# A decoder kernel on one core: the batch loop of both attention layers turned by half, and a key tile's second maximum placed behind the second head's scores

## What is computed

```
# layer 0: attention, no mask, two gates
aperture, expression = sigmoid(x @ Wa + ba), sigmoid(x @ We + be)       # per row and head
attn = softmax((x @ Wi) (x @ Wo)^T / sqrt(dh)) * aperture[q] * expression[k]
attn = attn / (attn.sum(-1) + 1e-8)
out  = rotate(attn @ (x @ Wv)) @ Wout          # a rotation and gains per head, folded into Wout
x    = layernorm(x + out)
# layer 1: attention of x over ctx, with a mask and biases
attn = softmax(where(mask == 0, -1e9, (x Wq^T + bq)(ctx Wk^T + bk)^T / sqrt(dh)))
x    = layernorm(x + (attn @ (ctx Wv^T + bv)) Wo^T + bo)
# layer 2: 16 experts with causal attention
...
```

## Time and profile before

| what | value |
|---|---|
| median of 3 runs | 4911.23 us |
| lowest, highest | 4908.39, 4921.2 us |
| the profiled execution | 4916.44 us, span 4914.7 us |
| TensorE busy, share of the span | 4307.2 us, 88% |
| VectorE, ScalarE, GpSimd busy | 2653.4 (54%), 1568.2 (32%), 902.7 us (18%) |
| granted clock of TensorE, mean | 0.935 |
| layer 0, layer 1, experts, about | to 1848, to 3845, to the end |

### The profile page before, as it was taken

How to read it: one execution, slowest core, us unless ns; L and a number is a source line. 1 busy time by engine, 2 the same in 40 slices (tenths; PEclk the granted TensorE clock), 3 DMA queues, 4 the chain that set the end, 5 groups by cost and what they waited for, 6 DMA issues and landing times. The chain is left out here.

```text
span 4914.7 us, 64052 instructions
## 1 busy us (share of the span) xinstructions
PE 4307.2 (88%) x22296; PEld 2467.3 (50%) x22296; DVE 2653.4 (54%) x3552; ACT 1568.2 (32%) x2813; POOL 902.7 (18%) x616
## 2 busy tenths in 40 slices
PE   5997899789879976999799979997999599989897
PEld 4443643454364434443544354435443376768686
DVE  3563465256345633664466445644664675757584
ACT  1453155225514531343134313431344202020302
POOL 3213311322132223102210221023101100000000
PEclk9999899899989997999899989998999799999898
DMA  3221322222122215210521052105210400010100
GB/s 84 67 65 50 80 47 61 69 65 46 46 83 67 53 37 159 61 40 27 168 61 40 27 168 61 40 27 163 65 40 18 140 18 35 18 35 7 46 1 18
DMA packets 120770, 294.79 MB, mean 60 GB/s; under 512 B 18352, under 2 KB 20272, under 8 KB 120432
## 3 DMA queue, kind: packets, MB, share of 16 engines
q1 hardware_dynamic: 93920, 222.20, 17.4%
q10 hardware_dynamic: 26512, 68.16, 4.1%
HBM read 145.87 MB, written 43.25 MB: 38 GB/s over the span
## 5 line engine op out<-in xcount | busy, mean ns | idle before, releaser
L869 ACT ACTIVATE probs<-half 128x512 f32<-128x512 f32 x2048 | 1113.2, 594 | 1176.0 <-PE half L682 679.8
L677 PE MATMUL half<-stack 97*128 97x512 f32 x2048 | 864.9, 487 | 9.9 <-ACT probs L869 5.6
L1044 DVE TENSOR_REDUCE mx<-wide 128x1 f32<-128x1024 f32 x512 | 603.0, 1220 | 443.2 <-PE wide L643 435.2
L1040 DVE CUSTOM_DVE_ANT_0 wide<-wide,mask_q 128x1024 f32<-128x1024 f32 x512 | 620.1, 1246 | 349.0 <-PE wide L643 341.4
L643 PE MATMUL wide<-stack 96*128 96x512 f32 x2048 | 630.5, 424 | 90.4 <-DMA stack<-qk 35.6
L677 PEld LDWEIGHTS half<-stack 97*128 97x128 f32 x2048 | 371.5, 192 | 600.9 <-issue 373.9
L609 PE MATMUL acc<-probs,v 128*32 128x512 f32 x4096 | 551.4, 609 | 2.9 <-ACT u L855 2.9
L587 PE MATMUL half<-stack,w 128*128 128x512 f32 x1536 | 388.6, 415 | 175.8 <-DVEq L953 151.7
L1386 PE MATMUL work_e<-w_in_e,x_e 128*128 128x512 f32 x2304 | 523.5, 389 | 0.0
L643 PEld LDWEIGHTS wide<-stack 96*128 96x128 f32 x2048 | 384.4, 192 | 200.4 <-DVE mx L1040 52.4
L1386 PEld LDWEIGHTS work_e<-w_in_e,x_e 128*128 128x128 f32 x2304 | 432.2, 188 | 89.7
(11 more groups left out here) (228 smaller groups left out, 3943.7 us busy)
## 6 DMA issues: line engine op xcount, KB each, us to landing
stack<-qk SPq DMA_DIRECT2D x384, 256.0 KB, 4.6
stage<-x_t SPq DMA_DIRECT2D x32, 512.0 KB, 3.5
k_raw<-x SPq DMA_DIRECT2D x8, 2048.0 KB, 9.3
x_t<-xts ACTq DMA_DIRECT2D x16, 1024.0 KB, 7.2
x<-k_raw ACTq DMA_DIRECT2D x8, 2048.0 KB, 8.6
mstage<-mask ACTq DMA_DIRECT2D x32, 512.0 KB, 3.6
mstage<-mask_t ACTq DMA_DIRECT2D x32, 512.0 KB, 3.6
over_a<-over_aperture SPq DMA_DIRECT2D x128, 64.0 KB, 2.7
```

Source lines behind the costliest of these rows:

```text
L677: last = pe.matmul(bank[:, :], stack[0:3 * DH + 1, s, 2 + h, kt * P:(kt + 1) * P], stack[0:3 * DH + 1, s, h, c * CH:(c + 1) * CH], start=T ...
L869: act.activation(probs[:, kt % 2 * 2 + h, c * CH:(c + 1) * CH], bank[:, :], ACT.Exp, scale=SCALE).then_inc(free, 1)
L1040: dve.tensor_tensor_reduce(bank[:, :], bank[:, :], mask_q[:, t, :], 1.0, -3e38, ALU.add, ALU.max, mx[:, p % 2, n:n + 1]).then_inc(free, 1)
L1044: dve.tensor_reduce(mx[:, p % 2, n:n + 1], bank[:, :], AX.X, ALU.max).then_inc(free, 1)
```

## The change

`attention_steps` is replaced by `pair_steps` and `section_steps`, which make three lists instead of one. Section 0 is the projections of batch 0. Section 1, in `Fori(0, B - 1)`, is the pair loop of batch i and then the projections of batch i + 1, woven with the end of batch i. Section 2 is the last pair loop and its end. `Section`, `Count` and `Ring` count, for each semaphore and buffer, how often it has been used up to a step of a section; they emit no instruction. The text of the engines is in a function `run(sec)` that goes through a section's list.

In the pair loop `MAXIMA` gives how many maxima stand in each tile, and only the first stands between the heads; the others (`late`) stand behind the second head's scores. `SLOT` gives each pair's place in `stack`: 0, 1, 2, 0, 1, 2, 1, 0. Pair 7's maxima but the last nine come ahead of pair 6's, and pair 7's stack ahead of pair 6's. Pairs 6 and 7 then have few or no maxima to work ahead on, and slots 1 and 2 become free for the next batch's x.

```diff
+SLOT = (0, 1, 2, 0, 1, 2, 1, 0)
...
+MAXIMA = ((2, 3, 3, 3, 3, 3, 2, 2),) + ((2,) * 8,) * 4 + ((2, 3, 3, 3, 3, 3, 1, 0), (2, 2, 2, 2, 1, 0, 0, 0), (0,) * 8)
...
+def pair_steps(masked, nxt):
+
+    units = lambda p: [("sm", p, h, t) for h in range(2) for t in range(TT)]
+    ahead = [m for p in range(1, 6) for m in units(p)] + units(7)[:7] + units(6) + units(7)[7:]
...
     for p in range(PAIRS):
         for kt in range(TT):
             before = (p, kt - 1) if kt else (p - 1, TT - 1)
+            if kt == 0 and p in (1, 2, 3, 4, 5):
+                steps.append(("stack", {1: 3, 2: 4, 3: 5, 4: 7, 5: 6}[p]))
+            if kt == 1 and p in (1, 3):
+                steps.append(("group", p // 2 + 2))
+            if nxt and kt == 1 and p == 5:
+                steps += [("load", "wv", 0), ("load", "wv", 1), ("split", "wv", 0), ("split", "wv", 1)]
+            if nxt and kt == 0 and p == 6:
+                steps += [("load", "xk", 0), ("load", "xk", 1)]
+                if masked:
+                    steps += [("mload", 0), ("mload", 1)]
+            if nxt and kt == 0 and p == 7:
+                for k in range(KT):
+                    steps.append(("split", "xk", k))
+                    if k < 2:
+                        steps.append(("load", "xk", k + 2))
             steps += [("st", p, kt, 0, c) for c in range(NC_)]
             misc = due
             due = []
...
-            spread = bool(ahead)
-            maxima(2 if p or kt else 0)
-            if not spread and before[0] >= 0:
+            rate = MAXIMA[p][kt]
+            late = []
+            for n in range(rate):
+                m = ahead.pop(0)
+                if n >= 1:
+                    late.append(m)
+                    continue
+                steps.append(m)
+                if m[2:] == (1, TT - 1):
+                    due.append(("mneg", m[1]))
+            if not rate and before[0] >= 0:
                 steps.append(("pv", *before, 0))
             steps += [("st", p, kt, 1, c) for c in range(NC_)]
             steps += misc
-            if p == 0 and kt:
-                maxima(1)
+            for m in late:
+                steps.append(m)
+                if m[2:] == (1, TT - 1):
+                    due.append(("mneg", m[1]))
...
+            if not masked and nxt and p == 7 and kt in (5, 6):
+                steps.append(("EX", kt - 5))
+            if masked and nxt and p == 7:
+                steps += [("mask", kt), ("mload", kt + 2)]
...
-    steps += [("out", t) for t in range(TT)]
-    steps += [("xt", t) for t in range(TT)]
...
+def section_steps(masked, att, nxt):
...
+    if att:
+        steps += pair_steps(masked, nxt)
+        steps.append(("res",))
+    else:
+        if masked:
+            steps += [("mload", 0), ("mload", 1)]
+        steps += [("load", "xk", 0), ("load", "wv", 0), ("split", "xk", 0), ("split", "wv", 0)]
+        steps += [("load", "xk", 1), ("load", "wv", 1), ("split", "xk", 1), ("split", "wv", 1)]
+        steps += [("load", "xk", 2), ("load", "xk", 3), ("split", "xk", 2), ("split", "xk", 3)]
+        if masked:
+            steps += [m for n in range(TT) for m in (("mask", n), ("mload", n + 2))]
+        else:
+            steps += [("turn_in",), ("EX", 0), ("EX", 1)]
...
+        for t in range(TT):
+            steps.append(("V", t))
+            if masked:
+                steps += [("mask", TT + t)] + ([("mload", TT + t + 2)] if t < TT - 2 else [])
+            steps += tail[t]
+        steps += [("load", "wk", 0), ("load", "wk", 1)]
...
+    if att:
+        if masked:
+            steps.append(("bo",))
+        steps += [("ct", t) for t in range(4)]
+        for t in range(TT):
+            if nxt and t < 2:
+                steps += [("split", "wk", t), ("load", "wq", t)]
+            steps.append(("out", t))
+            if t + 4 < TT:
+                steps.append(("ct", t + 4))
...
+        if masked:
+            steps += [("load", "xq", 0), ("load", "xq", 1)] + both("K", 0) + store
+            steps += both("K", 1) + both("K", 2) + both("K", 3)
+            for k in range(KT):
+                steps += [("split", "xq", k)] + ([("load", "xq", k + 2)] if k < 2 else [])
+            steps += [("xt", t) for t in range(HALF)] if att else []
+            steps += both("Q", 0) + stacked + both("Q", 1) + both("Q", 2)
+            steps += with_maxima(both("Q", 3) + [("CS", n) for n in range(4)], (3, 3, 3, 3, 2, 2))
+        else:
+            steps += both("K", 0) + store + both("K", 1) + both("Q", 0) + stacked + both("Q", 1) + both("K", 2)
+            steps += with_maxima(both("Q", 2) + both("K", 3) + both("Q", 3), (3, 3, 3, 3, 2, 2))
+        assert not first
+        steps += [("stack", 1), ("mneg", 0), ("row", 0)]
+        if att:
+            steps += [("xt", t) for t in range(HALF if masked else 0, TT)]
...
-        y = k_raw[:, :, :].rearrange("p g (a d) -> p (g a) d", d=D)
+        ct = sb("ct", [P, 4, 2, D], F32R, at=place["k_raw"])
...
+        y = sb("y", [P, TT, D], at=place["probs"])
+        wkv = sb("wkv", [P, 2, KT, D], F32R, at=place["qk"] if masked else None)
...
+                    elif kind == "res":
+                        sp.wait_ge(pv_done, blocks.upto(sec, ("pv", PAIRS - 1, TT - 1, 1)))
+                        alone(sp)
+                        sp.dma_start(y[:, :, :], io["res"][sec.batch, :, :].rearrange("b (t p) d -> p (b t) d", p=P))\
+                          .then_inc(res_in, 16)
...
-                    if kind == "out":
-                        pe.drain().then_inc(out_done, 1)
...
+            run(Section(0, None, False, True, lists[0]))
+            with dve.Fori(0, B - 1) as i:
+                run(Section(1, i, True, True, lists[1]))
+            run(Section(2, None, True, False, lists[2]))
```

1218 lines of the change are left out of this document (647 added, 571 removed).

## The result

The changed kernel took 5009.9 us (median, 5004.2 to 5016.3) against 4909.9 of the kernel before, a ratio of 1.020 (95% interval 1.0187 to 1.0212). It is 100 us slower where 41 less was forecast, and lies 75 us above the top of the stated range (4935). Its profiled execution has a span of 5014.3 us against 4914.7, so the two traces hold the whole difference.

A forecast was written before the change was run, and what follows sets the result against it. TensorE was taken as busy in key tiles and waiting in six inner boundaries, 1,003 us together. Layer 0's terms gave -8 and layer 1's -33, together -41 from 4911.2: 4870 us, range 4800 to 4935.

The forecast's parts named there:

- Tiles: Pair-loop key tiles: a maximum moved behind the second head's scores costs 0.46 us; +18.2 a batch in layer 0, +3.7 in layer 1.
- rival A: Pair-loop tiles: the late maximum is free, as the second head's exp holds `pv` anyway; 4776 us, chance 0.10.
- Tile 0 and the stall behind it: Start of a batch's pair loop: tile 0 costs about 3 us, gaining 7.9 in layer 0; layer 1 alike.
- New waits in the pair loop: Pair 5, for pair 6's stack and its row of negated maxima: 2.5 and 1.8 us in layer 0, 1 and 0.5 in layer 1.
- Boundary, layer 0: Between two pair loops of layer 0: 125 us, a gain of 34 each, three times: -102.
- C: Boundaries: GpSimd's queue of splits sets the pace, each gains 7 us less; no difference, 4911 us, chance 0.16.
- rival D: Boundaries: matmul groups behind waits run at the lower clock, 15 us a boundary; slower, 4960 us, chance 0.15.
- Boundary, layer 1: Between two pair loops of layer 1: 149.4 us, a gain of 26 each, three times: -78.
- first of layer 1: +12: Layer 1's first section: masks and their loads ahead of V cost 12 us (bounds 0 to 30).
- Layer 0's "+20": Layer 0's first section: K's weights waiting behind V, the gate's chain and added loop entry cost 20 us (bounds 5 and 40).
- The turn of the loop: End of each looped section, inside the boundary: 6.6 us a turn in layer 0, 7 in layer 1.
- Rival B: Loop turns: queues running ahead hide the turn, 6.6 us less at each of six; 4830 us, chance 0.05.

The follow-up runs named there:

- placement experiments: Changed kernel with two maxima between the heads again, 4925.8 us; kernel before with one between the heads, the others behind the second head's scores, 5001.1 us.
- CS experiments: Changed kernel with layer 1's column-sum steps moved: two ahead of Q's last units and the maxima, 4994.4 us; all four among the x splits before Q, 4981.1 us.
- best kernel: Layer 0 turned (two maxima between heads, two more of pair 7's ahead, later reciprocal, early K loads), layer 1 as before, both written out: 4809.1 us, ratio 0.9792.

## Why the prediction was wrong, step by step

Three parts of the sum failed. The pair loops were to cost 99 us in both layers and cost 174. Layer 1's boundaries were to gain 78 and gained 36. The stretch with layer 1's first section was to cost 8 and cost 37. The price of the moved maximum, which explains most of the 100 us against the kernel before, was right.

**Tiles: right.** "(1,1) 4.49, (1,2) 4.95" measured 4.50 and 5.02, "(1,1) 4.96" measured 4.96; rival A is out, by tiles and by both placement experiments. Layer 1's "(1,2) 5.42" measured 5.71: three maxima take VectorE 4.35 of those 5.7 us, and the third one's weights wait 0.45 for it (row at 2798.19), but I summed TensorE's rows alone. Ten such tiles in four batches are 12 us. As a part of the whole, the placement is 84 to 93 us, about what the sum held for it.

**Tile 0 and the stall behind it: too hopeful.** "Tile 0 costs about 3" in layer 0: tiles 0 and 1 took 11.6 us in the second batch against 15.9, a gain of 4.3 and not 7.9. "Tile 0 is alike" in layer 1 was wrong: it now has two maxima, and tiles 0 and 1 took 13.8 us against 10.0. Over all eight loops tiles 0 and 1 are 27 us longer than the forecast has them.

**New waits in the pair loop: in layer 0 the waits right, their price wrong.** 2.49 and 1.84 stand where 2.5 and 1.8 were forecast. What pair 5 cost wasn't 4.3 a batch in layer 0. Placement takes 15 of the 29 us that loop 2 grew, EX 7, tiles 0 and 1 gave 4 back: pair 5 has some 11. Moving the need for stack 6 alone gave back 28 us in both layers. The step that failed in layer 0 is that a wait was counted by its length; behind it matmuls ran at the lower clock (1.94 against 1.07). A part of the 11 is a wait that the forecast doesn't have: the 2.08 for VectorE in the tile with three maxima and a reciprocal, 2 to 3 us a batch by the run that moved it. In layer 1 the waits themselves were too small in the forecast: 1.5 and 1.7 where 1 and 0.5 stood, and 1.6 more in tile 2 for VectorE, which had no term.

**Boundary, layer 0: right.** 126.3, 125.1 and 121.2 for "125"; the outs ran at TensorE's pace. Rivals C and D didn't happen there.

**Boundary, layer 1: the sum was off by 14 each, and for other reasons than its terms.** V took 25 where 22 stood, the outs ended at 55 and not 50, the wait in front of Q was 9.4 with `xt` beside it and not 7, and the last stretch ran from 2508.77 to 2555.3, 46.5 us, where maxima, `CS`, row, half of `xt` and turn were forecast at about 40. The clock of 0.82 is hardly lower than before's 0.84; so this isn't rival D either, but VectorE-bound maxima with too few units beside them: before, they lay among eight V units. The CS experiments showed 15 to 29 us of it.

**Ends: "first of layer 1: +12" was the worst term.** It measured +37 with layer 0's end in it, +40 by itself. K waits 11.40 for weights whose load stands behind sixteen mask loads in SP's queue and whose split needs V's buffer free, Q 11.49, and the same maxima stretch comes here too; I priced the masks and not the queue behind them. Layer 0's "+20" was +26: K waits 10.5, its weights' load standing behind the folded weights' store (GpSimd's row at 80.17). The run with the loads ahead shows that the queue is the smaller part of both waits: K still waits 8.17 in layer 1 and 7.92 in layer 0, for a split that can't start before V's last unit has left the buffer. What holds Q for 11.49 no run tests by itself. The end of layer 1 grew by 10 where 12 was forecast.

**The turn of the loop: right in kind, 2 us too dear.** I put ScalarE's 6.6 us into the new boundary, and TensorE's row shows 4.40 there and 0.41 when written out. Rival B asked whether the turn hides: it doesn't, and the loops cost 66 us in the kernel before, turns and register waits together.

Of the 141 us between forecast and result, pair loops are 75, layer 1's boundaries 42, its first section with layer 0's end 29, layer 0's first section 6; the last stretch gave 8 back, 6 of them in the untouched experts, and layer 0's boundaries 4. By sign the outcome is the one that rival D names (4960), and even D is 50 us short. Its place is wrong: layer 0's boundaries gained what was forecast, and the largest miss is in the loops. Its mechanism, matmuls at the lower clock behind a short wait, is what pair 5 of layer 0 shows.

## What to carry to other kernels

When matmuls are moved within a pipelined tile, ask what the engine waits for at the old place: filler in front of a wait is free, and the same filler behind it costs its full time in every tile, here 0.47 us in each of 160 tiles of layer 0 (0.14 in layer 1, where the old place wasn't free either). Look at the rows behind a wait before you price it: four waits of 2.5 us with matmuls at the lower clock behind them cost 25 us, four of 1.5 us in layer 1 cost 5. A pipelined order across batches pays where the freed stretch was idle and nothing of what filled VectorE-bound parts is taken away: layer 0 gained 35 us a boundary, layer 1 12, and the best kernel turns only the first.
